# Turning the second normalised stream of a six-layer transformer with VectorE and DMA instead of TensorE

## What is computed

```
x = x + ln(attn(ln(x)))        # six layers: linear attention, then an MLP with LeakyReLU
x = x + ln(spiking(ln(x)))     # relu(x Wfc)^2 Wproj, then 5 threshold steps, spikes counted
x = x + ln(state_space(ln(x))) # project in, a convolution by FFT along the sequence, project out
x = x + ln(gated(ln(x)))       # a mix of x and x shifted by one token, key, gate, value

# one of the six layers of attn:
xn = layernorm(x, ln1_w, ln1_b);  q, k, v = xn @ wq, xn @ wk, xn @ wv
x  = linear_attention(softmax(q), softmax(k), v) @ wo + bo + x
xn = layernorm(x, ln2_w, ln2_b);  x = leaky(xn @ w1) @ w2 + x
```

## Time and profile before

| | |
|---|---|
| median of three runs | 845.98 us (844.92 to 846.48) |
| the profiled execution | 846.16 us |
| its span, first to last instruction | 844.3 us |
| TensorE busy | 791.0 us, 94% |
| VectorE busy | 662.4 us, 78% |
| ScalarE busy | 584.7 us, 69% |
| GpSimd busy | 462.1 us, 55% |
| DMA | 13.70 MB, 19729 packets |

### The profile page before, as it was taken

How to read it: one execution, slowest core, us unless ns; L and a number is a source line. 1 busy time by engine, 2 the same in 40 slices (tenths; PEclk the granted TensorE clock), 3 DMA queues, 4 the chain that set the end, 5 groups by cost and what they waited for, 6 DMA issues and landing times.

```text
span 844.3 us, 16194 instructions
## 1 busy us (share of the span) xinstructions
PE 791.0 (94%) x5354; PEld 687.8 (81%) x5354; DVE 662.4 (78%) x1937; ACT 584.7 (69%) x1244; POOL 462.1 (55%) x740
## 2 busy tenths in 40 slices
PE   7689999999999999999999999989999999998864
PEld 3468888999899989999899998878888887877752
DVE  4668788888788788788878787897875799999951
ACT  3466777787787777777777777778777657756353
POOL 6888556565576536544554445543454355566543
PEclk9799999999999999999999999999999999999996
DMA  9200000100000000100001000000000000000001
GB/s 258 94 0 2 1 1 1 39 1 2 1 26 14 2 2 1 38 2 1 1 2 39 1 1 1 1 1 3 1 1 1 2 1 2 2 14 26 14 14 38
DMA packets 19729, 13.70 MB, mean 16 GB/s; under 512 B 2488, under 2 KB 18495, under 8 KB 19647
## 3 DMA queue, kind: packets, MB, share of 16 engines
q1 hardware_dynamic: 19646, 12.67, 5.2%
HBM read 10.57 MB, written 2.10 MB: 15 GB/s over the span
## 4 chain that ended last, share of the span: by engine, by line
PE 76%; POOL 9%; DVE 7%; issue 4%; ACT 3%; DMA 0%; POOLq 0%; ACTq 0%; DVEq 0%
PE PS L317 68%; PE PS L327 8%; POOL XI L767 2%; ACT BIG L913 1%; POOL QB L877 1%; POOL RSTD L790 1%; POOL RSTD L797 1%; POOL RX L758 1%; ACT XR L956 1%; DVE QSM L1537 1%; DVE STATS L1273 1%; DVE STX L1258 1%; POOL R L725 1%; DVE ST L1194 0%; DVE XR L1315 0%
## 5 line engine op out<-in xcount | busy, mean ns | idle before, releaser
L317 PEld LDWEIGHTS PS<-W,HL 128*128 128x128 f32 x1536 | 194.1, 191 | 13.3 <-issue 5.3
L317 PE MATMUL PS<-W,HL 128*128 128x128 f32 x1536 | 202.0, 275 | 0.0
L969 ACT ACTIVATE HL<-PS 128x512 f32<-128x512 f32 x192 | 109.3, 593 | 14.5 <-PE PS L317 10.6
L779 POOL TENSOR_TENSOR JOIN<-STATS 128x8 f32<-128x8 f32 (+1 forms) x48 | 12.2, 254 | 159.0 <-DVE STATS L1273 159.0
L317 PE MATMUL PS<-X2H,W1L 128*128 128x512 f32 x192 | 91.6, 477 | 2.6 <-issue 2.2
L1138 ACT ACTIVATE EK<-PS,NKM 128x512 f32<-128x512 f32 x48 | 33.0, 688 | 76.7 <-DVE NKM L1498 76.7
L886 POOL TENSOR_TENSOR QB<-QB,QRC 128x512 f32<-128x512 f32 x48 | 50.9, 1061 | 56.5 <-DVE QRC L1540 56.5
L956 ACT ACTIVATE XR<-XI,RSTD 128x128 f32<-128x128 f32 x192 | 61.5, 393 | 25.4 <-POOL RSTD L797 25.3
L317 PE MATMUL PS<-X2H,W1H 128*128 128x512 f32 x192 | 76.2, 397 | 0.0
L317 PE MATMUL PS<-X2L,W1H 128*128 128x512 f32 x192 | 76.0, 396 | 0.0
L1273 DVE BATCH_NORM_STATS2 STATS<-XI 128x6 f32<-128x128 f32 x352 | 75.5, 277 | 0.1
(11 more groups left out here) (215 smaller groups left out, 2167.2 us busy)
## 6 DMA issues: line engine op xcount, KB each, us to landing
W<-in_w SPq DMA_DIRECT2D x12, 256.0 KB
X<-in_x SPq DMA_DIRECT2D x8, 256.0 KB, 4.6
out<-X SPq DMA_DIRECT2D x8, 256.0 KB, 2.3
QKV<-in_qkv SPq DMA_DIRECT2D x6, 192.0 KB, 2.8
FWD<-in_fwd SPq DMA_DIRECT2D x1, 1024.0 KB, 5.5
INV<-in_inv SPq DMA_DIRECT2D x1, 1024.0 KB, 8.1
WO<-in_wo SPq DMA_DIRECT2D x6, 64.0 KB
FWDX<-in_fwdx SPq DMA_DIRECT2D x1, 256.0 KB, 6.5
```

What stands on the lines that cost most here:

```text
L317: return nc.tensor.matmul(o, l, r, start=start, stop=stop, skip_group_check=True)
L969: nc.scalar.activation(HL[f][:, :], pH[f % 2][:, :], ACT.Prelu, alpha=LEAK).then_inc(s["hl"], 1)
```

## The change

It does these things together.

- **The turn.** `second_scale` moves from the head of VectorE's step to behind the statistics of item n-1. A new VectorE instruction, `second_blocks`, turns XR2 in 32x32 blocks into X2B, between `second_low` and `masked` (the mask to CT). A new function on SP moves the 16 blocks of a tile row and column with 16 DMAs of 32 partitions by 512 bytes, SBUF to SBUF, into X2D. `second_copy` reads X2D in a four-dimensional pattern, one step later than before (item n-3); `second_low` and the whole MLP move one step later too. TensorE's `second_turn` and its waits are gone.
- **GpSimd's order.** `first_root` (`ln1_power` before) comes ahead of the subtraction for the queries, `second_root` behind it.
- **SP's order.** A layer's weights are loaded in step b = 4 of the layer before it, behind that step's 16 transfers.
- **State-space kernel.** Three slices per step instead of two; the spectrum in the main steps (37 to 41) instead of steps 48 and 49.
- **Last sublayers.** `key` and `gate` use one weight each; the mix of the stream with its shift is made ahead of them (two ScalarE copies with a scale instead of one copy, and a new VectorE `blend` of two 128x512 instructions). Normalised results go to XI. The output projection's weights are centred in advance, and its normalisation needs no mean (two small GpSimd instructions less per sequence).
- **The end.** From step 44 on, `step` is not called: each engine has one straight list of calls, written out, in which the layers' operations and the later sublayers' are interleaved.

```diff
-SLICES = {DECAY + 3 + i: 2 * i for i in range(PAIRS // 2)}
-KERNEL_OUT = DECAY + 3 + PAIRS // 2
+SLICES = {DECAY + 3 + i: 3 * i for i in range(1 + PAIRS // 3)}
+KERNEL_OUT = DECAY + 4 + PAIRS // 3
-SPECTRUM = {ITEMS: (0, 1, 2, 3), ITEMS + 1: (4, 5, 6, 7, 8)}
+SPECTRUM = {CENTRE + 4 + i: (2 * i, 2 * i + 1)[:1 if i == TILES else 2] for i in range(TILES + 1)}
...
+            def second_turn(i):
+                sp.wait_ge(s["x2b"], i + 1)
+                if some(i):
+                    sp.wait_ge(s["x2h"], i)
+                for q in range(TILES):
+                    for c in range(TILES):
+                        sp.dma_start(X2D[32 * c:32 * (c + 1), q * P:(q + 1) * P],
+                                     X2B[32 * q:32 * (q + 1), c * P:(c + 1) * P]).then_inc(s["x2T_in"], 16)
+            def step(n, b, layer):
+                run(second_turn, n - 2)
+                if b == 4 and 1 <= layer < LAYERS - 1:
+                    sp.wait_ge(s["resid2"], layer * BATCH)
+                    sp.wait_ge(s["w_ready"], layer + 1)
+                    load(layer + 1, (layer + 1) % 2)
...
-            def second_turn(n):
-                pe.wait_ge(s["xr2"], n - 1)
-                ...
-                transposes(pX2, XR2).then_inc(s["x2T_ps"], 1)
...
+            def step(n, b, layer):
+                if n in SLICES:
+                    kernel_slice(SLICES[n])
+                run(turn, n)
+                run(hidden, n - 4, 2)
+                run(second, n - 4, 0)
+                ...
+                run(attend, n - 1)
+                run(keys, n)
+                run(second, n - 4, 1)
+                run(queries, n)
+                ...
+                run(hidden, n - 4, 3)
+                ...
+                run(weights_turn, n)
+                run(second, n - 4, 2)
+                run(context, n)
+                run(second, n - 4, 3)
+                run(values, n)
+                run(hidden, n - 3, 0)
+                if n in SLICES:
+                    kernel_slice(SLICES[n] + 2)
+                run(merge, n)
+                run(hidden, n - 3, 1)
...
+            def second_copy(i):
+                act.wait_ge(s["x2T_in"], BLOCKS * (i + 1))
+                if some(i):
+                    act.wait_ge(s["h_ps"], FB * i)
+                    act.wait_ge(s["x2l"], i)
+                affine(X2H, tokens(X2D), slot(i), 1)
+                affine(X2F, tokens(X2D), slot(i), 1).then_inc(s["x2h"], 1)
...
+                run(weights_copy, n)
+                run(second_copy, n - 3)
+                late_weights(n)
+                ...
+                run(context_copy, n)
+                run(queries_exp, n)
+                run(first_scale, n + 1)
...
+            def second_blocks(i):
+                dve.wait_ge(s["xr2"], i + 1)
+                if some(i):
+                    dve.wait_ge(s["x2T_in"], BLOCKS * i)
+                nc.vector.transpose(X2B[:, :].rearrange("p (c j r) -> p j c r", c=TILES, j=TILES), XR2[:, :]).then_inc(s["x2b"], 1)
...
+                run(second_stats, n - 1)
+                ...
+                run(second_scale, n - 2)
+                run(queries_blocks, n)
+                run(queries_max, n)
+                run(keys_reciprocal, n)
+                run(first_stats, n + 2)
+                ...
+                run(second_low, n - 3)
+                run(second_blocks, n - 2)
+                run(masked, n)
+                run(queries_sum, n)
...
+            def blend(v):
+                ...
+                stt(out=XK[:, :], in0=pX2[:, :], scalar=MU[:, 1:2], in1=SHK[:, 0:SEQ], op0=ALU.mult, op1=ALU.add)
+                stt(out=XM[:, :], in0=pX2[:, :], scalar=MU[:, 0:1], in1=SHR[:, 0:SEQ], op0=ALU.mult,
+                    op1=ALU.add).then_inc(s["blend"], 1)
...
             def key(v):
-                mm(pY[:, :], WK1[:, :], SH[:, 1:1 + SEQ], True, False)
-                mm(pY[:, :], WK2[:, :], SH[:, 0:SEQ], False, True).then_inc(s["k2_ps"], 1)
+                mm(pY[:, :], WKT[:, :], XK[:, :]).then_inc(s["k2_ps"], 1)
             def gate(v):
                 for j in range(TILES):
-                    mm(pXT[:, j * P:(j + 1) * P], SH[:, 1 + j * P:1 + (j + 1) * P], WR1[:, :], True, False)
-                    last = mm(pXT[:, j * P:(j + 1) * P], SH[:, j * P:(j + 1) * P], WR2[:, :], False, True)
+                    last = mm(pXT[:, j * P:(j + 1) * P], XM[:, j * P:(j + 1) * P], WRT[:, :])
...
             layers(step)
+            turn(44, ek_tm=44); hidden(40, 2, hl=161); second(40, 0, resid2=40); attend(43, q_fm=44)
+            keys(44, m_ready=44); second(40, 1); queries(44, resid1=44); hidden(40, 3, hl=162)
+            ...
+            shift_turn(7, blend=7); value(6, rv=6); gate(7, r_sig=7); key(7, rv=7); value(7, r_relu=8)
```

More of the change, by code:

```diff
@@ L28 @@
 STEPS = 5
+BLOCKS = 16 * TILES * TILES
 ITEMS = LAYERS * BATCH
@@ L358, in _, with freed @@
             pe.wait_ge(s["eighth"], 1)
-            def h(item, f):
-                w = item // BATCH % 2
-                if f == 0:
-                    pe.wait_ge(s["w1_lo"], item // BATCH + 1)
-                    pe.wait_ge(s["x2l"], item + 1)
-                k = item * FB + f
-                if some(k - 1):
-                    pe.wait_ge(s["hl"], k - 1)
+            def freed(name, count, readers):
+                if some(count) and not readers:
+                    pe.wait_ge(s[name], count)
@@ new lines, in weights_turn, with context @@
+            def weights_turn(i, **readers):
+                held(readers)
+                if late(i):
+                    freed("xTh", i + 1, readers)
+                pe.wait_ge(s["ek"], i + 1)
+                transposes(pXT, EK).then_inc(s["ekT_ps"], 1)
+            def context(i, **readers):
+                held(readers)
+                if late(i):
+                    freed("ek", i + 1, readers)
+                pe.wait_ge(s["ek_tm"], i + 1)
+                for j in range(TILES):
+                    last = mm(pK[:, 0:P], XR[:, j * P:(j + 1) * P], EKT[:, j * P:(j + 1) * P], j == 0, j == TILES - 1)
+                last.then_inc(s["g_ps"], 1)
@@ new lines, in _ @@
+            spiking_first(7, 1, relu=28); transform(3, 0, back=3); project_out(2, o_sum=2); transform(3, 1, back=3)
+            spiking_first(7, 2, relu=29); spiking_first(7, 3, relu=30); project_in(4, cnt_z=7)
+            state_turn(5, blend=1); spiking_second(7, 0, ym=7); spiking_second(7, 1); spiking_second(7, 2)
+            spiking_second(7, 3); inverse(3); key(0, o_sum=3); gate(0, u_sum=5); shift_turn(1, st_T=6)
+            count(7, r_sig=1); transform(4, 0, back=4); transform(4, 1, back=4); project_out(3, r_relu=1)
@@ new lines, in _ @@
+            project_in(5, cnt_z=8); inverse(4); state_turn(6, blend=2); project_in(6, u_sum=6); value(0, o_sum=4)
+            transform(5, 0, back=5); transform(5, 1, back=5); shift_turn(2, st_T=7); project_out(4, rv=1)
+            key(1, o_sum=5); inverse(5); gate(1, u_sum=7); project_out(5, r_relu=2); state_turn(7, blend=3)
+            transform(6, 0, back=6); transform(6, 1, back=6); key(2, o_sum=6); project_in(7, r_sig=2)
+            value(1, r_relu=3); inverse(6); gate(2, u_sum=8); shift_turn(3, st_T=8); project_out(6, rv=2)
@@ new lines, in _ @@
+            transform(7, 0, back=7); transform(7, 1, back=7); key(3, o_sum=7); shift_turn(4, blend=4)
+            gate(3, r_sig=3); value(2, r_relu=4); inverse(7); key(4, rv=3); gate(4, r_sig=4); value(3, r_relu=5)
+            project_out(7, rv=4); shift_turn(5, blend=5); value(4, o_sum=8); shift_turn(6, blend=6)
+            gate(5, r_sig=5); key(5, rv=5); key(6, r_relu=6); gate(6, r_sig=6); value(5, r_relu=7)
+            shift_turn(7, blend=7); value(6, rv=6); gate(7, r_sig=7); key(7, rv=7); value(7, r_relu=8)
@@ L769, in input_norm, with join_parts @@
                 last.then_inc(s["xi_init"], 1)
-            def join(first, end, turn):
+            def join_parts(first, end, turn):
                 def part(i):
@@ L1091, in gated_norm, with step @@
                 act.wait_ge(s["rv_nm"], v + 1)
[L1092 to L1099 removed]
+                normalise(seq(XI, v), ACC[:, :], RS[GATED], NMS[GATED]).then_inc(s["rv_z"], 1)
+            def step(n, b, layer):
                 if n in (KERNEL_OUT, KERNEL_OUT + 1):
@@ L1144, in step @@
-                if b == 0 and has_n:
-                    value_bias(layer)
-                if has_m:
-                    hl(m, 3)
-                at(n, 8, sigmoid)
-                if has_n:
-                    act.wait_ge(s["ekT_ps"], n + 1)
-                    copy(EKT[:, :], pXT[:, :]).then_inc(s["ek_tm"], 1)
-                at(n, 1, square, 1)
-                at(n, 7, shift_norm)
-                if has_x:
-                    second_copy(n)
+                run(rectified, n - 4, 2)
```

958 lines of the change are left out of this document (465 added, 493 removed).

## The result

The changed kernel takes 953.1 us (median of 4 runs, 952.55 to 954.3) against 845.64 us for the kernel before on the same chip: a ratio of 1.126, 95% interval 1.124 to 1.128. I had forecast 823 us. It is slower by 107.5 us. The profiled execution took 952.55 us, with a span of 950.8.

A forecast was written before the change was run, and what follows sets the result against it. TensorE was taken as the bound, busy 493.67 of the main part's 502.02 us. From 845.98 us, 1 us less there and 22 us less in the last part gave 823 us; own range 811 to 834, 8 in 10 806 to 858.

The forecast's parts named there:

- the pitch of the transfers: On SP's queue, time from one 32-row issue to the next, p: taken as 0.38 us, between 0.33 and 0.47.
- The ring's sum: From blocks through 16 issues, landing and copies to the next blocks: 3.0 + 15p + L, 11.0 us, under the step.
- Rival C: Transfers land late, ScalarE's X2H waits for DMA every step, the ring sets the step: 861 us, slower; chance 0.18.
- New turn: VectorE's turn of XR2 in 32x32 blocks, second_blocks: 0.71 us per item.
- X2H and X2F: ScalarE's two copies of the turned second stream, now read from SBUF: about 0.81 us each, 0.03 more.
- Landing: L, time from a transfer's issue until its data has landed in X2D: taken as 2.3 us.
- wrong outright: Stated failure sign: the main part changes by more than 18 us either way without a DMA wait.
- The main part: From the first turn of item 3 to that of item 44, 41 steps, 502.02 us: 1 us less forecast.
- a string to CT: EKT, X2H, X2F, X2L, blocks, CT before the merge product: TensorE keeps about 0.06 of 0.43 us, 2.5 us in all.
- The term for `second_scale` in the middle of the step: On VectorE, doesn't fit idle time in a layer's last step: five steps at 0.3 us, 1.5 us lost.
- The last part: From item 44's first turn on, 291.8 us: TensorE's work falls 12.9 us, idle time 9 us, together 22 us.
- the idle time: TensorE's 30.1 us idle in the last part: straight lists fill part of it, 9 us, to some 21 us.

The follow-up runs named there:

- twenty: The changed kernel with four more 32-row transfers per item, 20 issues instead of 16, into a tile nothing reads: 1067.5 us, main part 702.3 us.
- buffers_alone: The changed kernel with two buffers each of X2B and X2D and a landing count for each, VectorE's order kept: 951.8 us, main part 600.6 us.
- four_rows: The changed kernel with 4 transfers of 128 rows per item instead of 16 of 32, same bytes, no crossing of partitions: 854.4 us, main part 511.0 us.
- early_blocks: The changed kernel with X2B and X2D doubled, scaling at the head of VectorE's step, blocks behind the first stream's low part: 848.4 us, main part 502.1 us.
- merge_first: early_blocks with the second stream's scaling moved behind the scaled merge and the queries' blocks: 844.5 us, ratio 0.998 to the kernel before.
- turn_scale_early: The changed kernel with the turn back on TensorE, no transfers, and second_scale behind the queries' blocks: 860.2 us, main part 505.9 us.
- one_blend: early_blocks with one of the two blends left out, the gate reading the key's blend: 845.6 us, last part 289.3 us.
- order_alone: The changed kernel with VectorE's order as in early_blocks but single buffers of X2B and X2D: 1140.1 us, main part 772.2 us.
- probe: The kernel before with bursts of transfers, one shape each, on SP's idle queue behind the first loads: 847.0 us.

## Why the prediction was wrong

**The step that failed is the pitch of the transfers.** I took p = 0.38 us, between 0.33 and 0.47, "nearer to the one-row load by its count". Measured: 0.635 us (0.66 with the long issues), outside both ends. The reason behind the choice was false twice: between two ends in SBUF the number of rows doesn't count (1 to 128 rows, 0.59 to 0.60 us), and the rows I read the earlier trace rows were loads from HBM, while no transfer in that trace had both ends in SBUF. I had said so for the landing and not for the pitch. An unseen pair of ends should have had bounds as wide as a factor of two; a ring of 16 multiplies any error by 15.

**The ring's sum was right.** Rival C gave 3.0 + 15p + L. With the measured p = 0.635 and L = 1.8 that is 14.3 us. The long issues, about one in 27, stretch the mean burst from 15p = 9.5 to 9.9 us, which gives 14.7; the mean step is 599.7 / 41 = 14.63 us, and twenty confirms the slope. My forecast had the same sum and, by p, put the ring at 11.0 us, under the step. C named the place (ScalarE's `second_copy`, with GT behind it) and the sign, and had 0.18 of the chance; its price of 861 us came from p = 0.47. C also had the ring close through VectorE's order, which buffers_alone bore out. It was right in its mechanism; only the one term was too small.

**Right, point by point.** Turn gone from TensorE. New turn at 0.70 us (0.71), X2H and X2F at 0.81 and 0.80 (0.81). Landing 1.8 us, shorter than the 2.3 taken. (The prediction also tried a fixed 2.0 us for it. The Trainium skill, "DMA: Bandwidth & Descriptors", section "Anatomy of one DMA", gives that figure for DMAs that GpSimd issues; these came from SP.) X2H waits for a DMA in 40 of 41 steps, with the next one ring later: that was the sign I had given for C, and my line for "wrong outright" (over 18 us without a DMA wait) wasn't crossed; the change was 97.7 us with one.

**The main part without the ring.** I had forecast 1 us less, from a string to CT that would make TensorE wait before the merge product. That wait didn't come: in four_rows, with the change's own order, TensorE waited for CT 3 times in the whole run, 0.5 us each. With the change's own order and only 4 issues (four_rows) it is 9 us more; with better orders 0.1 us more (early_blocks) or 2.3 us less (merge_first). What ate the 10.9 us of work that TensorE lost were waits that I had no term for, for QS above all (9.3 us in early_blocks). The term for `second_scale` in the middle of the step, 1.5 us, was mis-sized: moving it alone gave back 4.6 us in turn_scale_early.

**The last part.** I had forecast 22 us less: 12.9 of work and 9 of idle time. The work fell by 10.5 us in early_blocks, somewhat less than forecast; key and gate took 19.5 us for 17.3 forecast. The step that failed is the idle time: it didn't fall by 9 but rose by 11.4 us, and the two cancel. Half of the rise lies between 734 and 824 us, where TensorE is busy for 69.0 of 90 us (74.6 before) and most of its waits end with VectorE. VectorE, at 90% in my sum, measured 82% (239.8 of 292.1 us), and 79.0 of those 90 us. But one_blend, with less work on VectorE, left TensorE's idle time as it was, so a full VectorE is not shown to be the cause; how much a better order of the lists would win there stays open.

## What to carry to other kernels

Before many small transfers take the place of an operation, find the price of one issue for exactly that pair of memories, and multiply: here 16 SBUF to SBUF issues were 10 us of a 12 us step, and their size didn't matter. Ask of every ring where it closes: through the buffers, through the queue, and through the in-order engine that both produces the next item and consumes this one; freeing one of these gave nothing (buffers_alone) or did harm (order_alone), freeing both gave 97.6 us. And work taken off a bound engine counts only if its waits don't grow by as much: here TensorE's work fell by 10.9 us in the main part and 10.5 us in the last, and its idle time rose by 11.0 and 11.4 us.

## What the runs showed of the hardware

- In probe, an issue on SP's queue took 0.59 us when both ends were in SBUF, 0.42 to 0.43 us from HBM to SBUF or back, with no difference between 1 and 128 rows SBUF to SBUF. Landing was 1.8 us for 16 KB. The Trainium skill, "DMA: Bandwidth & Descriptors", section "Issuing engines are not separate DMA queues", says that the time to initiate a DMA "is usually small relative to the DMA itself"; here one issue was a third of the landing, and the 16 of an item (10 us) were over five times it.
- 29 of the change's 768 issues took 0.9 to 1.9 us, and 2 of the probe's 96 took 1.1 and 1.6 us; why was not found.
- The scaling XR <- XI,RSTD took 1.23 us beside a GpSimd multiplication in SBUF and 0.65 us clear of it. That agrees with the Trainium skill, "SBUF — State Buffer", section "Who interferes with whom": a VectorE instruction with two SBUF inputs contends with a GpSimd instruction that reads SBUF. In the change, with a GpSimd instruction of 128x8 beside it (JOIN <- STATS), it took 0.67 us. Two places in a list were worth 0.29 us an item on average.
- While TensorE waited in nearly every step, the granted clock of the main part was 0.95 (0.99 in early_blocks, 1.00 before), and its busy time for the same 3359 matmuls 518 us (483 us in early_blocks). The first product of `h`, most of which comes soon behind the wait, took 0.51 us on average against 0.46; a matmul of `y`, which comes ahead of it, 0.275 us in both.
